# A decoder layer with routed experts: one admission number per tile, empty tiles admitted as a group, experts' loads and counting moved, and two orders changed inside the turns

## The reference

```
x = x + attn(layernorm(x))     # 4 heads of 64 ... exp features of 128, causal linear attention, @ Wo,
                               # layernorm(batch + attn), then relu(h @ W1 + b1) @ W2 + b2, W1: 256 x 1024
x = x + cross(layernorm(x), ctx)   # q, k, v of 256; softmax(q k / 16) v, within a sequence
x = x + ffn(layernorm(x))      # 16 experts of width 176, the best 2 of each row
    probs = softmax(xf @ Wg.T); topw, topi = top_k(probs, 2); topw /= topw.sum()
    out = sum over the two: gate * ((silu(xf @ W1[e]) * (xf @ W3[e])) @ W2[e])
```

## Time and profile before

| what | value |
|---|---|
| median of 3 runs | 912.8 us (911.93 to 912.94) |
| profiled execution | 915.41 us, its span 913.6 us |
| mean granted clock of TensorE | 0.944 |
| busy: PE, PEld, DVE, ACT, POOL | 815.8, 735.0, 611.8, 394.4, 408.8 us |
| bytes moved by DMA | 133.17 MB, mean 146 GB/s |

### The profile page before, as it was taken

One profiled execution on the slowest core, in us unless ns is written; L12 is line 12 of the kernel. 1 busy time (PEld: TensorE's weight loads), 2 busy tenths in 40 slices (PEclk: granted clock), 3 DMA queues, 4 the chain that ended last, 5 costly groups with the idle time before them and its releaser, 6 DMA issues.

```text
span 913.6 us, 19931 instructions
## 1 busy us (share of the span) xinstructions
PE 815.8 (89%) x5660; PEld 735.0 (80%) x5661; DVE 611.8 (67%) x1725; ACT 394.4 (43%) x1070; POOL 408.8 (45%) x585
## 2 busy tenths in 40 slices
PE   6899999999999999999999999998632999999970
PEld 6788999899999999898999899997521788888860
DVE  4446677788778887787877878766646655555540
ACT  4252543626446254452644526444133444444440
POOL 4212133352543525435244353441646466667661
PEclk9899999999999999999999999998655999999995
DMA  8960054370633706336063360709722577767756
GB/s 265 347 237 2 31 201 155 101 249 18 241 139 115 252 14 241 126 128 240 26 243 128 126 232 22 243 30 271 160 74 76 93 122 119 119 122 123 121 79 199
DMA packets 89699, 133.17 MB, mean 146 GB/s; under 512 B 6464, under 2 KB 54272, under 8 KB 89408
## 3 DMA queue, kind: packets, MB, share of 16 engines
q1 hardware_dynamic: 64352, 103.03, 34.0%
q0 software_dynamic: 14944, 19.69, 12.4%
q10 hardware_dynamic: 10368, 10.03, 4.4%
HBM read 37.70 MB, written 99.23 MB: 150 GB/s over the span
## 4 chain that ended last, share of the span: by engine, by line
PE 55%; ACT 15%; DVE 14%; issue 7%; POOL 3%; DMA 1%; SPq 0%; ACTq 0%; DVEq 0%; POOLq 0%
PE ps L685 47%; ACT phi L1102 5%; PE ps L692 4%; ACT fT_hi L1115 4%; ACT relu_v L1116 3%; PE ps L985 2%; PE ps L999 2%; DVE nmax L1414 1%; DVE xrow_full L1449 1%; DVE smax L1456 1%; DVE row_max_of L1458 1%; DVE prT_lo L1309 1%; ACT pr L1158 1%; POOL row_sums L676 1%; ACT qT_hi L1137 1%
## 5 line engine op out<-in xcount | busy, mean ns | idle before, releaser
L676 POOL DMA_INDIRECT row_sums<-narrow,sidx x80 | 124.3, 1554 | 66.4 <-issue 20.1
L685 PE MATMUL ps<-e_sb,narrow 128*128 x320 | 109.4, 465 | 1.1 <-DVE narrow L1646 1.1
L1102 ACT ACTIVATE phi<-ps,nmax 128x128 f32<-128x128 f32 x256 | 71.3, 380 | 21.8 <-DVE nmax L1414 21.7
L685 PE MATMUL ps<-w_hi,fT_hi 128*128 128x256 f32 x256 | 78.3, 306 | 2.0 <-DVE fT_lo L1309 1.9
L685 PE MATMUL ps<-hT_hi,w_hi 128*128 128x256 f32 x256 | 73.3, 286 | 1.5 <-DVE hT_lo L1309 1.5
L685 PE MATMUL ps<-hT_lo,w_hi 128*128 128x256 f32 x256 | 72.6, 283 | 0.0
L685 PE MATMUL ps<-hT_hi,w_lo 128*128 128x256 f32 x256 | 72.5, 283 | 0.0
L1309 DVE TENSOR_TENSOR fT_lo<-relu_v,fT_hi 128x512 fp32r<-128x512 f32 x64 | 52.5, 820 | 29.7 <-ACT relu_v L1116 29.7
L685 PE MATMUL ps<-w_hi,fT_lo 128*128 128x256 f32 x256 | 72.2, 282 | 0.0
L685 PE MATMUL ps<-w_lo,fT_hi 128*128 128x256 f32 x256 | 72.1, 282 | 0.0
L685 PEld LDWEIGHTS ps<-e_sb,narrow 128*128 128x128 f32 x320 | 55.0, 192 | 19.4 <-issue 2.7
(11 more groups left out here) (284 smaller groups left out, 2712.9 us busy)
## 6 DMA issues: line engine op xcount, KB each, us to landing
expert_rows<-zero_rows SPq DMA_DIRECT2D x16, 4352.0 KB, 16.0
narrow<-expert_rows ACTq DMA_DIRECT2D x72, 136.0 KB
e_sb<-in_E SPq DMA_DIRECT2D x4, 1408.0 KB, 11.7
X<-in_x SPq DMA_DIRECT2D x16, 256.0 KB, 3.0
ctx_raw<-in_ctxT SPq DMA_DIRECT2D x16, 256.0 KB, 16.0
row_sums<-X SPq DMA_DIRECT2D x16, 256.0 KB, 2.2
out<-row_sums SPq DMA_DIRECT2D x16, 256.0 KB, 5.5
raw_w<-in_W SPq DMA_DIRECT2D x2, 1024.0 KB, 6.5
```

The source lines that it names most:

```text
L676: pool.indirect_dma_start(sum_dram, bass.IndirectOffsetOnAxis(sidx[:, u:u + 1], 0), yg[:, u, :], None, compute_op=ALU.add).then_inc(scatte ...
L685: return pe.matmul(out_, lhsT, rhs, start=start, stop=stop)
L1102: last = act.activation(phi[:, g, h, :], ps[:, g, h * M:(h + 1) * M], ACT.Exp, bias=nmax[:, g, h:h + 1])
```

## The change

Nine edits, told by engine. SP: the experts' loads take the zeros of e2b from zero_rows by DMA, without a wait for a fill; e2a has its own semaphore. The admission of a tile loads one number: added_need now has one row, which for a tile that meets the tile one or two back, or whose next tile meets the tile before it, asks for the add one tile back. Slot 72 (`SURE`) waits for the three adds before it only if it holds rows, by late_need; slots 73 to 79 load one number each and don't wait for three back. Before the copy of the sums one number is loaded for all eight buffers; if slot 72 is empty it asks for the adds up to slot 71 only. GpSimd: the fill of e2b is gone; `place_rows` waits for the rows, gates and zeroed bands itself; in turn 17 it stands where it does in other turns; the last sequence's rows are copied by ScalarE. TensorE: in turn 17 the router's transposes and products of sequence 14 come earlier, and `count_choices` behind the transposes of pr; in all turns with a feed-forward and an attention part, two of the four steps of `ffn_out(1, ...)` move from behind the score products to ahead of the prT product; e2_ready is awaited in slot 1 instead of ahead of the tiles. ScalarE: `e2a_first` is in turn 17 behind qT, `e2_rounded(0)` and `(1)` behind the counts. VectorE: `hidden` and `row_max` of groups 2 and 3 alternate; the choice of sequence 14 is made ahead of the score maximum; five `e2_rest` lie in turn 17, three behind the plan.

The core of the diff:

```diff
@@ sync
                 sp.wait_ge(w2_ps, NSEQ)
-                load(e2a[1].bitcast(F32), E2[:, 0:P, :].rearrange("e p d -> p e d"), e2_loaded)
-                sp.wait_ge(e2b_zero, 1)
+                load(e2a[1].bitcast(F32), E2[:, 0:P, :].rearrange("e p d -> p e d"), e2a_loaded)
+                load(e2b[IR:LO].bitcast(F32), zero_rows[IR:LO, 0:D].unsqueeze(1).broadcast_to([LO - IR, NE, D]), e2_loaded)
...
+            def number(at, low):
+                return sp.value_load(at, min_val=low, max_val=16 * (SLOT_TILES // GB + 1))
 
             def slot_tiles(s, u, last):
-                early = s if isinstance(s, int) and s < ADDING else ADDING
                 if isinstance(s, int) and s == 1:
                     sp.wait_ge(ranges_ready, 1)
-                if early == ADDING and not last:
-                    v = (u - ADDING) % GB
-                    hold(sp, scattered[v], rows_added(s - ADDING, v))
-                near = range(1, (ADDING if last else min(early, ADDING - 1)) + 1)
-                needs = [need_of(k, s) for k in near]
-                for k, need in zip(near, needs):
-                    hold(sp, scattered[(u - k) % GB], need)
+                if isinstance(s, int) and s == SURE:
+                    need = number(late_need[0:1, 0:1], 16 * (SURE // GB))
+                    for k in range(1, ADDING + 1):
+                        hold(sp, scattered[(u - k) % GB], need)
+                elif not first(s):
+                    if not last and not (isinstance(s, int) and s < ADDING):
+                        v = (u - ADDING) % GB
+                        hold(sp, scattered[v], rows_added(s - ADDING, v))
+                    need = number(added_need[0:1, bass.ds(s, 1)], 16)
+                    hold(sp, scattered[(u - 1) % GB], need)
                 sp.sem_inc(may_add)
...
+            need = number(late_need[0:1, 1:2], 16 * (SURE // GB + 1))
             for u in range(GB):
-                need = sp.value_load(landed_need[0:1, u:u + 1], min_val=16 * (NT * TOPK // GB + 1),
-                                     max_val=16 * (SLOT_TILES // GB + 1))
                 hold(sp, scattered[u], need)
@@ gpsimd
-                if last_cross:
-                    place_rows(r)
                     store_rows(r)
...
                 if last_ffn:
-                    pool.wait_ge(w2_ps, NSEQ)
-                    pool.wait_ge(rstd_ready[3], b + 1)
-                    pool.memset(e2b[P // 4:LO].bitcast(F32), 0.0).then_inc(e2b_zero, 1)
-                    pool.wait_ge(e2b_zero, 1)
                     place_rows(r)
@@ tensor
                     turn_tiles(7, pr).then_inc(prT_ps, 1)
+                if last_cross:
+                    count_choices()
...
+                if f is not None and not last_ffn:
+                    ffn_out(1, 0, 2)
                 if b is not None:
                     pe.wait_ge(prT_ready, b + 1)
...
-                    ffn_out(1, 0, FC // 2)
+                    ffn_out(1, 2, FC // 2)
@@ vector
-                if f is not None and not last_ffn:
-                    hidden(2)
-                    hidden(3)
-                if a is not None:
-                    row_max(2)
-                    row_max(3)
+                for g in (2, 3):
+                    if f is not None and not last_ffn:
+                        hidden(g)
+                    if a is not None:
+                        row_max(g)
...
+                if last_cross:
+                    for q in range(2):
+                        e2_rest(q)
...
+                if last_cross:
+                    for q in range(2, 5):
+                        e2_rest(q)
...
-            for q in range(3):
-                e2_rest(q)
...
-            for q in range(3, 8):
-                e2_rest(q)
...
+                then(dve.tensor_tensor(meeting[:, 0, 2:], meeting[:, 0, 2:], meeting[:, 1, 2:], ALU.max))
+                then(dve.tensor_tensor(meeting[:, 0, 1:SURE], meeting[:, 0, 1:SURE], meeting[:, 1, 2:SURE + 1], ALU.max))
+                last = dve.scalar_tensor_tensor(added_need[:, 1:SURE], meeting[:, 0, 1:SURE], 16.0, round_of[:, 0:SURE - 1],
+                                                ALU.mult, ALU.add)
                 last.then_inc(ranges_ready, 1)
 
+            for q in range(5, 8):
+                e2_rest(q)
```

More of the change, by code:

```diff
@@ L578, in keep_rows @@
                     hold(pool, placed, r * 16 * TOPK * TS)
[L579 to L582, removed]
+                pool.tensor_copy(kept[:, :, :, D], row_no[:, tiles_of(r)].unsqueeze(2).broadcast_to([P, TS, TOPK]))\
+                    .then_inc(ids_kept, 1)
+                if not own:
+                    hold(pool, xn3_ready, r + 1)
+                    pool.tensor_copy(kept[:, :, :, 0:D], xn3.unsqueeze(2).broadcast_to([P, TS, TOPK, D]))\
+                        .then_inc(rows_kept, 1)
             def store_rows(r):
@@ L630, in turn @@
                     keep_rows(r)
-                if r is not None and not last_ffn and not last_cross:
+                if r is not None and not last_ffn:
                     place_rows(r)
@@ L636, in turn @@
                     root(3, b, eps_ln)
-                if r is not None and not last_ffn and not last_cross:
-                    store_rows(r)
-                if last_cross:
-                    place_rows(r)
+                if r is not None and not last_ffn:
                     store_rows(r)
@@ L824, in turn @@
                 if last_cross:
[L825 removed]
+                    router(b - 1, 1)
                 if f is not None:
@@ L1139, in turn @@
                 if last_cross:
-                    copy_router_rows(b - 1, 0)
+                    act.wait_ge(e2a_loaded, 16)
+                    for q in range(4):
+                        e2a_first(q)
                 if a is not None:
@@ L1182, in turn @@
                     features(3)
-                if r is not None and not last_ffn and not last_cross:
+                if r is not None and not last_ffn and not last_cross and not last_turn:
                     choice_counts(r)
@@ L1210, in turn @@
                     act.mul(xwq[0], bank(6), SCORE_SCALE).then_inc(split_hi, 1)
-                if last_cross:
-                    act.wait_ge(e2_loaded, 16 * 3)
-                    for q in range(4):
-                        e2a_first(q)
                 if last_turn:
-                    for q in range(2):
-                        e2_rounded(q)
+                    for j in range(TOPK):
+                        last = copy(rows_last[:, :, j, 0:D], xn3)
+                    last.then_inc(rows_kept, 1)
+                    choice_counts(r)
                     for q in range(4):
@@ L1615, in _ @@
                                   ALU.not_equal)
-            dve.scalar_tensor_tensor(added_need[:, ADDING - 1, ADDING:], real[:, ADDING:], 16.0,
-                                     round_of[:, 0:SLOT_TILES - ADDING], ALU.mult, ALU.add)
-            then(dve.tensor_tensor(real_late[:, :], real[:, SLOT_TILES - 2 * GB:SLOT_TILES - GB], real[:, SLOT_TILES - GB:],
-                                   ALU.add))
-            then(dve.tensor_scalar(landed_need[:, :], real_late[:, :], 16.0, float(16 * (NT * TOPK // GB + 1)),
-                                   ALU.mult, ALU.add))
+            dve.scalar_tensor_tensor(added_need[:, SURE + 1:], real[:, SURE + 1:], 16.0,
+                                     round_of[:, SURE:SLOT_TILES - 1], ALU.mult, ALU.add)
+            for n in range(2):
+                last = dve.tensor_scalar(late_need[:, n:n + 1], real[:, SURE:SURE + 1], 16.0, float(16 * (SURE // GB + n)),
+                                         ALU.mult, ALU.add)
+            then(last)
             def meeting_tiles():
```

45 lines of the change are left out of this document (22 added, 23 removed).

## The result

The changed kernel takes 890.3 us (median of 4 runs, 889.9 to 890.5) against 912.4 us in the runs of the kernel before on the same chip: a ratio of 0.976, 95% interval 0.9743 to 0.9777. It is 22 us faster. 37.8 were forecast, and the time lies above the range of 866 to 888. The profiled execution took 889.92 us, its span is 888.2; the one of before was 3 us longer than its median, so the spans differ by 25.4.

The account below looks back on a forecast made before the run. TensorE was taken to bound the turns and tiles, a chain of small steps the hand-over, SP's loads and the copy the end. Gains 12 + 9.5 - 0.5 + 16.8 = 37.8 off 912.8 gave 875.0 us, range 866 to 888.

Parts of the forecast that it names:

- Turns: Steady turns: VectorE's new order and the moved feed-forward products save 0.85 us a turn, 12 us in all, bounds 0 and 15.
- Hand-over: From the turns to the expert tiles: four edits on a chain of small steps gain 9.5 us, bounds 6 and 12.
- step (b): Between turns and tiles: GpSimd places sequence 13 3.5 us earlier, so its four writes land and turn 17 comes 3.8 to 4.4 earlier.
- (a): Between turns and tiles: e2b's fill on GpSimd, 3.50 us, goes, with VectorE's stretched norm; 3.2 us off the chain into turn 17.
- (c): Turn 17: sequence 14 is counted ahead of TensorE's wait for prT, so the last sequence finds GpSimd free: 4.7 us.
- (d): Ahead of the plan: VectorE's e2 subtractions, 4.77 us for the last four, leave the path for waits in turn 17.
- the rule of the Trainium skill that the prediction weighed: Turn 17: VectorE operations with two SBUF inputs make GpSimd's reads wait; 1.5 to 3 us lost, 878 us, chance 0.06.
- Tiles: Expert tiles: admission by one number makes nine tiles wait for the one before, lag covered by the buffers; 0.5 us lost.
- Behind the last tile: After the last tile: fewer loads and waits on SP start the copy at 876.7, not 897.2; gain 16.8, bounds 12 and 20.5.
- the 22 that it had named as a sign of being wrong: At the end: the forecast would be wrong if the copy took over 22 us from its first issue.
- the 20.1 of the sum: At the end: DMA time of the copy, 12.6, and of six empty adds, about 7.5, taken as the copy's length.
- Rival 1: At the end: the copy starts early but shares DMA badly, gain 12 there, 880 us; chance 0.12.

Follow-up runs that it names:

- e2b_later: The changed kernel with the two loads of e2b held until the four writes of sequence 13 have landed: 885.7 us, 0.9715 of the kernel before.
- two_numbers: The changed kernel with two admission numbers a tile for tiles 1 to 71, as before the change: 885.6 us, 0.9693 of the kernel before.
- both: The changed kernel with two admission numbers a tile and the e2b loads behind the landing of sequence 13's writes: 882.0 us, 0.967 of the kernel before.

## Why the prediction was wrong, step by step

**Turns: right, a little low.** Both gaps, their cause and their removal were as described; nothing took their place. They were read as 1.07 us together, and 0.85 was booked for the fear that VectorE's chain would hold some back; the period fell by 1.06 (38.03 to 36.97 between the products with prT_hi), and the start to A by 15.3, the upper bound. The last number is loose: in the ten traces of kernels that keep the new order A lies between 624.6 and 628.0. With both edits undone 14.2 of it come back. The split's part was read rightly as cover for prT_lo, but not that it would be idle cover.

**Hand-over, step (b): failed.** It said that the four writes of sequence 13, started 3.5 us earlier, would land 3.8 to 4.4 us earlier, and that "the earlier e2b loads run beside these writes as before". GpSimd's index was 3.3 us earlier (635.5 against 654.1 less 15.3), but the landing was 1.3 earlier and the product behind it 0.5. The 7.41 us in the earlier trace rows was read as the writes' own time. It was a queue: e2b_later gives 2.4 us from the last issue, and the DMA engines of the kernel before stood at a share of 1.05 to 1.11 from 655 to 665. What is shifted into a queue lands when the queue is empty: 23.2 us behind A, against 24.5 before. The queue's end moved so little although its loads did not run "as before": without the fill to wait for, those of e2b were issued 2.85 us behind A instead of 9.05. That filled the 2.8 us (649.5 to 652.3) in which the engines had been idle before, but the zeros of e2b are now a transfer too. From A to 28 us behind it the engines moved 4.8 MB instead of 4.5, and their share times its length comes to 23.8 us instead of 19.9. The prediction booked nothing for the zeros' DMA; no run takes it away, so its own part stays open.

**Steps (a), (c), (d): right.** The fill's 3.5 us arrived at the issue of the writes (636.62, 9.7 behind A, against 655.38, 13.2 behind) and were lost only behind it, in step (b). From the product with prT_hi to the last index the kernel gained 4.2 us (4.7 forecast), and the plan's subtractions are off the path. The small GpSimd operations beside VectorE's subtractions are slowed here too (1.30 us in the row at 652.00, beside two of them from 652.02 to 654.38, against 0.22). By the rule of the Trainium skill that the prediction weighed (SBUF — State Buffer, Who interferes with whom) the trace agrees; it was not the term that decided.

**Tiles: the lag was right, its price not.** Chained adds 4.8 apart and one stall of 0.5 came as forecast. What was missed is that lag does not end when it is covered. From scaling to add it is 14.4 us at tile 22, 6.8 at tile 43, 13.1 at tile 45 after the next two chained adds, and still 5.7 at tile 71: it shrinks by 0.36 us a tile at best, 0.28 on average from 45 to 71. Of the 1.4 us lost from C to D that stall is 0.5, and the profile of the changed kernel run again does not have it; 0.4 are the longer wait in the first tiles (1.43 us, and 1.05 with two numbers); the rest stays open. Another part, 0.9 us in the first tile, has no experiment behind it; the traces show the granted clock at 0.50 for 5.1 us from B on (to 687.2), against 3.5 before (to 706.0), and the first four products taking 2.7 us instead of 2.4.

**Behind the last tile: the term that was mis-sized.** The prediction had the copy start 11.2 us ahead of the last scaling and take 20.1; it was 3.8 and 22.3, over the 22 that it had named as a sign of being wrong. The first error is 7.4 us: "its add starts at 871.2", 0.6 after the scaling, where the trace of before already had that add at 875.5, released by SP:

```profile
875.52 1.55 POOL L676 DMA_INDIRECT row_sums<-narrow,sidx  x1 [1.16 <-SPq L475]
```

SP was to have admitted tile 71 18.4 us ahead of D (869.5); the kernel before did so at 13.2, the changed kernel at 12.1, and two_numbers at 15.3. So of these 6.3 us the stricter number made 3.2, and the rest was a lag that the prediction left at nothing. The other 1.1 are SP's own nine steps, 8.3 us and not 7.2. The second error is 2.2 us, and two errors partly cancel in it. All DMA work had landed 18.4 us behind the copy's first issue (884.2), 1.7 sooner than the 20.1 of the sum; but the end is not the sum. Behind the last add, which took 11 us from issue to landing, stand another 3.9 us, the drain, which the trace of before showed only where it cost nothing and for which the prediction has no term. The prediction quoted the Trainium skill (DMA: Bandwidth & Descriptors, Queues, rings and completion order) for taking turns between queues. The trace agrees as far as both queues move packets from 880.0 to 883.35 (87 of the copy's, 176 of the adds'). But what the prediction drew from it, that the last add would not stand behind the whole copy, did not come: it landed behind the copy's last packet (883.3). Rival 1, the early copy with poor sharing, was the nearest; it put the loss at 5 us, and 9.6 was measured, most of it from the late start.

## What to carry to other kernels

A landing time read from a trace is the transfer's own only if the DMA engines were not full; look at their share over the same stretch before you book an earlier issue as an earlier landing. A lag that the buffers hide is still there at the end of a loop, and sets when the next stage may start: take the start of the epilogue from the lagging queue's own rows. When two edits remove the same wait, undo each and both, and don't add their gains.

## What the runs showed of the hardware

- GpSimd's closing drain ends 3.7 us after its last indirect add has landed (900.0 against 896.3 before, 887.9 against 884.2 changed), and the kernel ends 0.2 us later where nothing else is open (887.9 and 888.2).
- Loads of 48 partitions kept the 16 DMA engines at a full share at 100 to 160 GB/s (in e2b_later, with no other transfer issued beside them, 145 GB/s at a share of 1.16 from 647.0 to 653.8), where a load of 128 partitions ran at 350 to 390.
- Indirect writes of 128 rows that land in 2.4 us on free engines (e2b_later) took 9.5 beside such loads (changed). Indirect adds took up to 9.7 us (both) or 11 (changed) beside a copy within DRAM, against 3.9; the copy's last packet came 17.5 us behind its first issue instead of 15.2.
